# A convolution's first group reordered, and three entries of a slot table moved, in a fused four-layer Trainium2 kernel

## The reference

```python
def reference(x, ...):
    x = L0(x)   # channel attention: softmax(max - q q^T) q, mixed with x by a squeeze-excite gate
    x = L1(x)   # 1x1 reduce, depthwise 3x3, FFT attention and FFT filter, 1x1 post, + x
    x = L2(x)   # group norm, 8-head self-attention over 256 pixels, projection, + x
    x = L3(x)   # three 3x3 convolutions q, k, v; attention across the 16 images at each pixel;
                # layer norm, relu, a fourth 3x3 convolution, + x
    return x
```

## Time and profile before

| what | value |
|---|---|
| median of three runs | 499.68 us |
| the profiled execution, its own time | 500.01 us |
| its span, first to last instruction | 498.2 us |
| TensorE busy | 465.4 us, 93% of the span |
| VectorE busy | 344.7 us, 69% |
| ScalarE busy | 249.3 us, 50% |
| GpSimd busy | 126.4 us, 25% |
| mean granted TensorE clock | 0.974 of full |
| share of TensorE in the chain that ended last | 71% (VectorE 13%, ScalarE 6%) |

### The profile page before, as it was taken

How to read it: one execution, slowest core, us unless ns; L and a number is a source line. 1 busy time by engine, 2 the same in 40 slices (tenths; PEclk the granted TensorE clock), 3 DMA queues, 4 the chain that set the end, 5 groups by cost and what they waited for, 6 DMA issues and landing times.

```text
span 498.2 us, 10552 instructions
## 1 busy us (share of the span) xinstructions
PE 465.4 (93%) x3790; PEld 374.0 (75%) x3790; DVE 344.7 (69%) x890; ACT 249.3 (50%) x590; POOL 126.4 (25%) x154
## 2 busy tenths in 40 slices
PE   7999999988998999899899989999996999998896
PEld 6877765767586778677776867777774789898895
DVE  1448578867687787788777876876476442776895
ACT  3424756645555555555556455534633431294551
POOL 6022443474012112201120121120110011332762
PEclk9999999898899999999999999999997999998998
DMA  7100012030001001000100000000000000005112
GB/s 271 45 22 2 1 49 91 1 91 23 0 6 44 18 0 42 21 0 0 42 21 0 12 9 0 2 23 1 0 1 22 1 22 2 1 1 168 44 50 77
DMA packets 10639, 15.28 MB, mean 31 GB/s; under 512 B 624, under 2 KB 8944, under 8 KB 10480
## 3 DMA queue, kind: packets, MB, share of 16 engines
q1 hardware_dynamic: 10608, 14.86, 9.3%
HBM read 10.66 MB, written 4.19 MB: 30 GB/s over the span
## 4 chain that ended last, share of the span: by engine, by line
PE 71%; DVE 13%; ACT 6%; issue 4%; POOL 3%; DMA 1%; DVEq 0%; SPq 0%; ACTq 0%; POOLq 0%
PE bank L1232 10%; PE bank L1233 8%; PE bank L1234 8%; PE bank L1345 5%; PE bank L1437 5%; PE bank L1374 5%; PE bank L1411 3%; PE bank L1239 3%; PE bank L1409 2%; PE bank L1465 2%; PE bank L1452 2%; PE bank L1249 2%; DVE nmax L1007 1%; PE bank L1261 1%; PE bank L1297 1%
## 5 line engine op out<-in xcount | busy, mean ns | idle before, releaser
L1232 PE MATMUL bank<-win,w_hi 128*128 128x256 f32 x384 | 117.2, 305 | 2.6 <-POOL win L592 1.2
L1233 PE MATMUL bank<-win,w_hi 128*128 128x256 f32 x384 | 108.9, 284 | 0.0
L1234 PE MATMUL bank<-win,w_lo 128*128 128x256 f32 x384 | 108.7, 283 | 0.0
L751 ACT ACTIVATE prob<-bank 128x512 f32<-128x512 f32 x128 | 69.5, 596 | 69.7 <-PE bank L1409 69.0
L1007 DVE TENSOR_REDUCE nmax<-bank 128x2 f32<-128x512 f32 x128 | 84.9, 687 | 18.8 <-PE bank L1374 18.4
L1232 PEld LDWEIGHTS bank<-win,w_hi 128*128 128x128 f32 x384 | 73.1, 190 | 9.5 <-issue 1.6
L1233 PEld LDWEIGHTS bank<-win,w_hi 128*128 128x128 f32 x384 | 73.3, 191 | 0.4
L1234 PEld LDWEIGHTS bank<-win,w_lo 128*128 128x128 f32 x384 | 73.1, 190 | 0.0
L540 POOL TENSOR_TENSOR first<-first 128x256 f32<-128x256 f32 x24 | 17.7, 737 | 152.7 <-ACT first L643 152.7
L1239 PE MATMUL bank<-ones_r 128*128 128x256 f32 x276 | 50.0, 319 | 1.1 <-DVE ones_r L856 1.1
L1374 PE MATMUL bank<-qk 32*128 32x256 f32 x256 | 33.0, 335 | 12.7 <-DVE nmax L1007 7.2
(11 more groups left out here) (240 smaller groups left out, 900.0 us busy)
## 6 DMA issues: line engine op xcount, KB each, us to landing
w_stage<-convs SPq DMA_DIRECT2D x4, 576.0 KB, 4.0
x_t<-x_px SPq DMA_DIRECT2D x8, 256.0 KB, 3.1
x_in<-x SPq DMA_DIRECT2D x8, 256.0 KB, 2.8
out<-x_pair SPq DMA_DIRECT2D x8, 256.0 KB, 2.2
q<-out SPq DMA_DIRECT2D x1, 2048.0 KB, 8.4
out<-v SPq DMA_DIRECT2D x8, 256.0 KB, 2.1
cst<-small SPq DMA_DIRECT2D x1, 1712.0 KB, 9.1
cst<-small SPq DMA_DIRECT2D x1, 253.5 KB, 3.5
```

Of the source, the lines that this page charges most:

```text
L751: act.activation(prob[:, x // 4 % 2, x % 4, :, :], bank[ST_BANK[x % 2]][:, :], ACT.Exp, scale=L2_SCALE).then_inc(st_exp, 1)
L1232: mm(dst, hi, x_hi, start=(row == 0), stop=False)
L1233: mm(dst, hi, x_lo, start=False, stop=False)
L1234: return mm(dst, lo, x_hi, start=False, stop=(row == KH - 1))
```

## The change

The constants move three things. On VectorE `make_window(m=1)` goes from slot 10 to slot 11, on ScalarE `window_high(m=1)` from slot 11 to slot 12, and on GpSimd `diff0` from slot 12 to slot 14. On TensorE the first three units of each pair's convolution become `first_mix`: six products of high inputs, a wait for `win_low`, and then the three products of low inputs. The wait ahead of the convolution is now for `win_high`. All products and their number stay the same.

```diff
-POOL_SLOTS = {"rn": 1, "squares": 8, "diff0": 12, "grstd": 18}
+POOL_SLOTS = {"rn": 1, "squares": 8, "diff0": 14, "grstd": 18}
...
-WINDOW_SLOTS, ADD_SLOT, RESIDUAL_SLOT, HIGH_SLOTS, LOW_SLOTS = (3, 10), 6, 7, (8, 11), (11, 12)
+WINDOW_SLOTS, ADD_SLOT, RESIDUAL_SLOT, HIGH_SLOTS, LOW_SLOTS = (3, 11), 6, 7, (8, 12), (11, 12)
...
+            def first_mix(w, slot, dst, j):
+
+                hi, lo = conv_weights(w)
+                o = POS[0] * KC
+                for row in range(KH):
+                    x_hi = win_hi[slot][:, 0, :, row:row + H, :]
+                    mm(dst[:, 0:HW], hi[:, o + row * C:o + row * C + C], x_hi, start=(row == 0), stop=False)
+                    mm(dst[:, 0:HW], lo[:, o + row * C:o + row * C + C], x_hi, start=False, stop=False)
+                pe.wait_ge(win_low, 2 * j + 2)
+                for row in range(KH):
+                    mm(dst[:, 0:HW], hi[:, o + row * C:o + row * C + C], win_lo[slot][:, 0, :, row:row + H, :],
+                       start=False, stop=(row == KH - 1))
...
                     if u == 0:
-                        pe.wait_ge(win_low, 2 * j + 2)
+                        pe.wait_ge(win_high, 2 * j + 2)
...
+                    if u < KH:
+                        if u == 0:
+                            first_mix(0, win_slot(j), bank[conv_bank(j, 0)][:, :], j)
+                        continue
                     ins = product(g // 2, win_slot(j), bank[conv_bank(j, g)][:, :], g, k)
```

## The result

In the runs made right after the prediction the changed kernel took 491.87 us (median of 4 runs, 491.0 to 492.1), the kernel before 499.4 us (4 runs, 498.23 to 499.95): ratio 0.9846, 95% interval 0.9815 to 0.9877. That is 7.5 us, where 5.0 were forecast. The time lies 0.1 us above the lower end of the range. A repeat in a later session gave less, 0.9893 (0.9859 to 0.9928), 4.9 us between medians; the two intervals overlap. The mean of all ten runs of the changed kernel is 492.6 us, that of all 86 of the kernel before 498.7 us, so 6.1 us between them is the best single number on record. Lines of TensorE's helpers have moved: L1374 is now L1387, L1409 and L1411 are L1422 and L1424, and `first_mix` is L1242 and L1243 (high inputs) and L1246 (low inputs).

A forecast was written before the change was run, and what follows sets the result against it. TensorE, busy 93% of the span, was taken as the bound, so gains come from its idle time or clock. Terms summed to 5.0 us off 500.01, 495.0, less 0.3 for the runs' median: 494.7 us, range 491.8 to 497.1.

The forecast's parts named there:

- Rivals D and E: D: clock falls once in each loop pass, 501.5 us, chance 0.03; E: saved wait met again one slot later, 499.7, 0.05.
- Loop passes, 0.70 each: Slot 12's scores lose their 0.77 us wait for VectorE's maximum; each of four passes gains 0.70 us.
- Last convolution, 0.72: Last pair: TensorE starts on high parts at 408.69 instead of 409.41, gaining 0.72 us.
- Pair 1, 0.5: Slot 12's wait of 0.55 us; gain taken as 0.5, since GpSimd's weight mixing hardly lets the maximum of step 13 move.
- pair 0, zero: diff0 goes behind the weight mixing; any gain ends where TensorE waits for ScalarE, so zero.
- Pair 6: TensorE at half clock, too late to wait in slot 12: zero gain, upside under 1 us with a better clock.
- Pair 7, 0.98: Slot 12's scores start at 379.89 instead of 380.87, gain 0.98 us, as if the half-clock stretch moved with the idle.
- rival C: Better clock in pair 7: the half-clock fall doesn't come, at most 3.4 us more saved, 491.3 us; chance 0.08.
- The sum: 4 x 0.70 + 0.5 + 0.98 + 0.72 = 5.0 us over loop passes, pairs 1 and 7, last convolution.
- inner bound of 496.3: Slow end of the forecast itself: the skill's full lock, half of pair 7's gain, none of pair 1's.
- The lock: Slots 11 to 14: VectorE's window_low and GpSimd's diff0 exclude each other, first one winning; window_low(m=1) ends 0.47 us after diff0.

## Why the prediction was right, and where it was wrong

**Direction and mechanism: right.** Every sign of being right that the prediction listed under "What would show it" is in the trace: no wait for a maximum in slot 12, `diff0` ahead of the second `window_low`, that one 1.07 us long, L939 at 0.29, slot 14 without a wait in the loop, the last convolution behind the high parts. Rivals D and E did not occur; no half-clock stretch lies inside the loop.

**Loop passes, 0.70 each: right.** Four periods went from 180.80 to 178.02 us (mean of both profiles), 2.8 for 2.8.

**Last convolution, 0.72: right.** 0.73 by the wait, 0.75 by the order alone against the whole change.

**Pair 1, 0.5, and pair 0, zero: right, pair 1 a little high.** From slot 10 of pair 1 to that of pair 2, with one half-clock stretch of 3.4 us in it each time, it is 49.19 and 49.17 us in two profiles of the old order and 48.80 to 48.84 in six of the new: 0.37. From a common row in pair 0 (62.07 in the kernel before run again, 61.77 in the changed one) to slot 10 of pair 2 it is 91.42 against 90.86, 0.56. The 0.19 between the two lie in pair 0, where profiles of either order differ by 0.3 us at full clock, and are not shown to come from the change.

**Pair 6, "zero, with an upside of under 1 us if the clock is better": the step that failed.** It measured 0.93. I had read from one execution that TensorE came too late in slot 12 to wait. That execution had a half-clock stretch just there, and the other profile of the same kernel has none and waits 0.88 us. With the stretch pair 6 took 42.88 us, without it 42.28. The usual state of the pair is that of a loop pass, and the term should have been 0.7 or more. The "upside of under 1 us" named the right size; what was wrong was to take the one execution's clock for the usual one and to put the term at zero.

**Pair 7, 0.98: about right, by an argument that was too simple.** With the last convolution it measured 2.1 between the first two profiles and 1.8 between the means of all, so 1.4 or 1.0 for slot 12. At full clock it is 0.72. The rest is clock. Slot 12 waits 1.17 us for the exponentials, as the 1.2 of the prediction, but starts only 0.51 us earlier behind slot 10 (2.40 us, before 2.91), because in the changed kernel the stretch already covers slot 10's scores (in two profiles of the new order where it begins behind them, it is 1.97 us). More comes back between slots 12 and 14 (4.52 us, before 5.24). I had counted the half-clock stretch as all or nothing (rival C, 3.4 us); it stayed (rival C fell), but it costs more the more TensorE is busy in it: 4.81 us of 6.8 in the changed kernel, 5.82 in the one before. That is not the whole of it, since two profiles of the old order are as little busy (4.79 and 4.82) and still take 1.6 and 1.8 us longer than the new. Why the stretch begins 0.8 us ahead of slot 10 in four of the six profiles of the new order without dummies, and behind it in all four of the old, was not settled.

**The sum.** 0.37 + 2.78 + 0.93 + 1.8 = 5.9 us, where I had 5.0; the excess is pair 6. It fits the 6.1 us between the means of all runs. As a ratio it is 0.988: inside the repeat's interval (0.9859 to 0.9928) and just outside the first one's (0.9815 to 0.9877). What is left, some 1.6 us between 5.9 and 7.5, I put down to few runs: the kernel before lay at 499.4 for 4 runs and at 498.0 to 498.95 in three later sessions of 11 to 30, and the changed one at 491.87 for 4 runs and at 493.11 for 6. Those 4 runs had a mean granted clock of 0.986, the 6 of the repeat 0.983; by the runs of the kernel before (2.6 us between 0.990 and 0.979) I estimate 0.7 us for that. The rest is argued from the spread; no experiment settles it. My range was also drawn around a median of three runs as if it were exact, which moved it some 1 us up. Its inner bound of 496.3 for the forecast itself is a slip: the terms named there give 496.5.

**The lock.** That whichever engine is first holds the other off was right in both directions. The Trainium skill, "SBUF — State Buffer", section "Who interferes with whom", has the blocked instruction wait for the whole of the other. The rule for who blocks agrees with the trace, in both directions. The second `window_low` ended 0.55 us after `diff0` did (202.68 and 202.13), where the rule at its word gives 0.68 and I gave 0.47; with `diff0` held back, where the maximum came 0.4 us earlier still, the periods did not change, so the difference was worth nothing.

## What to carry to other kernels

When a term of a sum is read as zero because "the engine was late there anyway", look whether that lateness is the usual one; a half-clock stretch in the one profiled execution can hide a wait that most executions have. When an instruction is moved on one engine, look whether the engine that consumes its result has to take it later too; otherwise the wait may only change its name (here from the maximum to `even`, and a pass got 0.3 us longer). And where a few dummy products fit into idle time ahead of a half-clock stretch, they can be worth more than a term of a reordering: by the profiles 1.1 us here for 14 products in one pair, and 2.4 us in the kernel before for 21.

## What the runs showed that I had not expected

The head of the program, from the start of the span to slot 10 of pair 2, took from 151.35 to 156.43 us in fourteen profiles, 5.1 us apart and so almost as much as the change is worth, and not by kernel: the longest was the old order with dummies 220 us later, the shortest the changed kernel with dummies. Two things vary in it: TensorE's first wait for constants from memory (0.71 to 2.54 us) and its time at half clock behind that, from none (twice) to 10.2 us. This is the spread of the runs, and cutting the timeline at common rows removes it: the four periods of one order differ by under 0.2 us between all profiles.

Pair 7, where TensorE stands waiting 1.0, 1.2 and 1.2 us (in the old order 2.2) one after the other, had a half-clock stretch in every profile in which the waits were left open, and none in two of the three in which dummies filled them (3.4 us in the third). Loop passes, with waits of 0.70 and 0.77 us, never had one in any of the fourteen profiles.
